# A macaron layer on one core: row statistics, one residual and three small steps take other places at the stages' changes

## The chip, the cores and the metric

The kernel runs on one core of one Trainium2 chip. Its time is the device time of one execution in microseconds (us). Five engines work side by side, each with a queue of its own that is served in order: TensorE (PE, matrix multiplies and transposes), VectorE (DVE), ScalarE (ACT), GpSimd (POOL) and SyncE (SP, which here only issues DMAs). They wait for one another by semaphores, and the program writes every wait by hand. The matrix products are float32 products made of three products of a high and a low half each.

## The reference

Input x has 8 batches of 1024 rows of 128 features (8192 rows).

```python
x = x + 0.5 * ffn(layernorm(x), ...)      # mixture of 16 experts, the best 4 by row, and a shared one
x = x + attn(layernorm(x), w_q, w_k, w_v) # rotary, causal, 1 head of 128, per batch of 1024 rows
x = x + 0.5 * ffn(layernorm(x), ...)      # the same weights again

# ffn: scores = sigmoid(x @ gate_w.T); the top 4 of scores + gate_b; their scores normed, times 2.5
#      y = sum over e of c_e * ((silu(x @ w1_e.T) * (x @ w3_e.T)) @ w2_e.T), plus the shared expert
# layernorm: (x - mean) / sqrt(var + 1e-5), over the 128 features
```

## The kernel before

The layer runs as three stages on the whole core: the first ffn over 16 tiles of 512 rows (T = 0 to 15), attention over 8 batches of 8 query blocks of 128 rows, the second ffn over 16 tiles (T = 16 to 31 in the semaphores' counts). Features lie on the partitions in the ffns, rows in attention.

A tile of an ffn is nine steps j: eight pairs of experts and the shared expert. In step j TensorE makes the gate product and the up product of pair j (`ffn_up`, three 512-column matmuls each) and, three steps behind, the down product of pair j-3 (`ffn_down`). ScalarE takes silu of the gate, VectorE multiplies it by the row weights (`ffn_weighted`, L1316) and by the up product (`ffn_h`, L1326), ScalarE rounds that to the high half (`ffn_h_hi`, L857) and GpSimd subtracts it for the low half (`low_half`, L633). A gate product waits until `ffn_weighted` of two steps earlier has left its PSUM bank, an up product until `ffn_h` has left its own.

Beside that each tile prepares the next ones. The sums of a tile's rows and of their squares (mean and variance) come three or four tiles ahead, from VectorE (`ffn_stats`, `ffn_mv`) or, for most tiles, from ScalarE (`ffn_means`, `ffn_vars`, L885 and L894). GpSimd makes the root (`ffn_rows`) and takes the mean off (`ffn_center`), VectorE scales (`ffn_scale`, L1203), ScalarE and VectorE split it (`ffn_xh`, `ffn_xl`, L1196), and TensorE makes the router's logits of the next tile (`ffn_logitsT`). ScalarE copies them out (`ffn_logitsT` of its own), VectorE chooses the experts and transposes the weights (`ffn_combT`, L1305), and SP writes these to DRAM and loads them back, spread over all partitions, by ten DMAs per tile in five groups (`comb_rows`, L462 and L473). `ffn_weighted` waits for the group that holds its pair.

The opening (tile 0) is written out by hand in `ffn_start` of each engine and the `start` branches of `ffn_tile`: weights are still split, row weights of the first four pairs go by `comb_spread` over TensorE, and TensorE fills waits with multiplies of zeros (`warm`). TensorE runs gates 0 to 5, then the logits of tile 1. VectorE makes the statistics of tiles 0 to 3, that of tile 3 between `ffn_xl` of tile 1 and `ffn_weighted` 2.

In tile 14 the first batch of attention is prepared: GpSimd makes root and shift (`attn_shift`, four operations) behind the low half of step 2, ScalarE applies them to eight blocks (`attn_xn`, L955), two blocks a step in steps 4 to 7, and TensorE transposes the first four (L2075) in step 6.

In attention, query block i of a batch goes through scores, `attn_max` (L1668, VectorE), `attn_exp` (ScalarE), `attn_probT` (TensorE transposes, ScalarE copies), `attn_pv` (TensorE) and `attn_residual` (L1679, VectorE). `attn_pv` of block i waits for `attn_residual` of block i-1. In the last batch the routing of the second ffn's first tile (T = 16) runs between these steps on VectorE (`ffn_prep`), and `ffn_combT` of that tile ends it.

## Time and profile before

| | us |
|---|---|
| median of three runs | 816.37 |
| lowest, highest | 814.94, 819.16 |
| the profiled execution's own time | 816.33 |
| its span (first to last instruction) | 814.5 |
| TensorE busy | 802.5 (99%) |
| VectorE busy | 722.9 (89%) |
| GpSimd busy | 615.2 (76%) |
| ScalarE busy | 600.1 (74%) |

The span divides into the first ffn (to about 312 us), attention (to about 510 us) and the second ffn. A matmul of 512 columns is drawn with a length of 0.39 us while the next one starts 0.23 us behind it, so "busy" is close to full even where a short wait stands between two of them; the timeline's bracket gives only the part of a wait that lies beyond the drawn end.

### The profile page before, as it was taken

The page shows a single profiled execution, that of the slowest core. Times are in us where ns is not written, and L with a number is a line of the kernel's source. Part 1 is how long each engine was busy: PE and PEld are TensorE (multiplying, and loading weights), DVE is VectorE, ACT ScalarE, POOL GpSimd, SP SyncE. Part 2 cuts the span into 40 slices and gives each one's busy share as a digit, 9 for nine tenths or more (in the row PEclk, how much of TensorE's full clock was granted, in tenths as well). Part 3 has the DMA queues.
Part 4 walks back from the last instruction along what each step waited for, and adds up shares of the span by engine and source line. Part 5 has one row for each costly group of instructions (what it writes and reads, how often), then busy time and mean ns, then how long its engine had stood idle before and what let it go on. Part 6 is the DMA issues. An engine that isn't in the chain of part 4 may idle for free. (4 is left out here: it accounts for less than half of the span.)

```text
span 814.5 us, 15848 instructions
## 1 busy us (share of the span) xinstructions
PE 802.5 (99%) x4066; PEld 657.1 (81%) x4066; DVE 722.9 (89%) x2027; ACT 600.1 (74%) x1495; POOL 615.2 (76%) x560
## 2 busy tenths in 40 slices
PE   8999999999999999999999999999999999999998
PEld 7677777777778767899999998777777777777887
DVE  6899999999999988788888888789999999999986
ACT  5777788888786677776676766778788778886664
POOL 6777777777777679888888884477777777777764
PEclk9999999999999999999999999999999999999999
DMA  7567788878877746643333450556676776666653
GB/s 231 137 175 210 211 246 237 243 233 243 219 207 209 206 123 163 159 140 83 100 96 112 145 150 20 159 148 188 183 201 194 195 202 197 179 177 173 184 143 94
DMA packets 93480, 140.83 MB, mean 173 GB/s; under 512 B 10352, under 2 KB 39648, under 8 KB 93408
## 3 DMA queue, kind: packets, MB, share of 16 engines
q1 hardware_dynamic: 93408, 140.03, 61.6%
q8 instruction: 25, 0.41, 0.2%
q14 instruction: 47, 0.39, 0.1%
HBM read 112.67 MB, written 18.93 MB: 162 GB/s over the span
## 5 line engine op out<-in xcount | busy, mean ns | idle before, releaser
L633 POOL TENSOR_TENSOR h_l<-probT,h_h 128x512 fp32r<-128x512 f32 x254 | 330.0, 1302 | 137.4 <-ACT h_h L857 135.1
L857 ACT ACTIVATE h_h<-probT 128x512 fp32r<-128x512 f32 (+1 forms) x285 | 179.4, 629 | 58.2 <-DVE probT L1326 28.6
L1798 PE MATMUL bank<-xh,w_h 128*128 128x512 f32 x545 | 218.7, 401 | 2.4 <-DVE prob L1316 1.4
L1798 PE MATMUL bank<-xh,w_l 128*128 128x512 f32 x545 | 214.2, 393 | 0.0
L1798 PE MATMUL bank<-xl,w_h 128*128 128x512 f32 x545 | 213.8, 392 | 0.0
L920 ACT ACTIVATE bank<-bank 128x512 f32<-128x512 f32 x252 | 146.2, 580 | 68.5 <-PE bank L1798 65.9
L1326 DVE TENSOR_TENSOR probT<-prob,bank 128x512 f32<-128x512 f32 x255 | 172.6, 677 | 15.3 <-POOL h_l L633 3.6
L1316 DVE TENSOR_TENSOR prob<-bank,qkT 128x512 f32<-128x512 f32 x252 | 171.3, 680 | 15.6 <-ACT bank L920 11.2
L1798 PEld LDWEIGHTS bank<-xh,w_h 128*128 128x128 f32 x545 | 102.3, 188 | 40.5 <-DVE probT L1329 7.2
L1798 PEld LDWEIGHTS bank<-xh,w_l 128*128 128x128 f32 x545 | 102.3, 188 | 23.3
L1798 PEld LDWEIGHTS bank<-xl,w_h 128*128 128x128 f32 x545 | 102.3, 188 | 21.2
L1798 PE MATMUL bank<-h_h,w_h 128*128 128x512 f32 (+1 forms) x297 | 113.7, 388 | 0.2 <-POOL h_l L633 0.2
L1798 PE MATMUL bank<-h_h,w_l 128*128 128x512 f32 (+2 forms) x297 | 113.8, 388 | 0.0
L1798 PE MATMUL bank<-h_l,w_h 128*128 128x512 f32 (+1 forms) x264 | 101.0, 387 | 0.0
L857 ACT ACTIVATE probT<-bank 128x512 f32<-128x512 f32 (+2 forms) x96 | 44.4, 489 | 49.2 <-PE bank L2124 49.2
L1798 PE MATMUL bank<-stage,probT 128*128 128x128 f32 x576 | 76.4, 278 | 0.8 <-DVE X L1679 0.5
L1798 PEld LDWEIGHTS bank<-stage,probT 128*128 128x128 f32 x576 | 70.8, 191 | 5.8 <-DVE X L1679 1.8
L1798 PEld LDWEIGHTS bank<-h_h,w_h 128*128 128x128 f32 x297 | 55.5, 188 | 16.8 <-POOL h_l L633 1.5
L1798 PE MATMUL bank<-qkT 128*128 128x512 f32 (+4 forms) x288 | 65.3, 353 | 0.5 <-issue 0.5
L1798 PEld LDWEIGHTS bank<-h_h,w_l 128*128 128x128 f32 (+1 forms) x297 | 55.2, 188 | 11.0
L1798 PEld LDWEIGHTS bank<-h_l,w_h 128*128 128x128 f32 x264 | 49.2, 188 | 10.6
L633 POOL TENSOR_TENSOR qkT<-rot,qkT 128x512 fp32r<-128x512 f32 x32 | 43.5, 1371 | 11.5 <-ACT qkT L857 11.5
(143 smaller groups left out, 1340.5 us busy)
## 6 DMA issues: line engine op xcount, KB each, us to landing
qkT<-comb_rows SPq DMA_DIRECT2D x190, 256.0 KB, 5.2
qkT<-comb_rows SPq DMA_DIRECT2D x124, 128.0 KB, 3.0
rows<-comb_rows SPq DMA_DIRECT2D x28, 512.0 KB, 7.1
stage<-stage SPq DMA_DIRECT2D x64, 128.0 KB, 3.0
X<-in_x SPq DMA_DIRECT2D x16, 256.0 KB, 3.1
stage<-in_x_t SPq DMA_DIRECT2D x16, 256.0 KB, 6.7
x_t<-stage SPq DMA_DIRECT2D x16, 256.0 KB, 4.5
X<-x_rows SPq DMA_DIRECT2D x64, 64.0 KB, 5.8
```

The costliest lines, as they stand in the source:

```text
L633: nc.gpsimd.tensor_tensor(lo, f, hi.bitcast(F32), ALU.subtract).then_inc(done, 1)
L857: return nc.scalar.activation(dst, src, ACT.Copy)
L920: nc.scalar.activation(bank[:, G_BANK[g], :], bank[:, G_BANK[g], :], ACT.Silu).then_inc(silu_done, 1)
L1316: nc.vector.tensor_tensor(weighted[j % 2], bank[:, G_BANK[(q + j) % 2], :], comb_b[q][:, j, :], ALU.mult).then_inc(weighted_done, 1)
L1326: nc.vector.tensor_tensor(h_place(T, q, j), weighted[j % 2], bank[:, u, :], ALU.mult).then_inc(h_done, 1)
L1798: return nc.tensor.matmul(dst, lhsT, rhs, start=start, stop=stop)
```

## The change

- Opening: the statistics of tile 3 leave VectorE. ScalarE makes its means between the copy of the down weights and `comb_spread(2)`, and its variances in two halves around the copy of tile 1's logits. They go to a small tile of their own, `mv_3`. TensorE takes tile 1's logits ahead of gate 5 instead of behind it.
- End of tile 0: VectorE makes `ffn_xl` of tile 2 ahead of its product of step 8, not behind it.
- Tile 14: `attn_shift` stands behind the low half of step 1, not 2, and `attn_xn` runs in steps 3 to 6, not 4 to 7.
- Last batch of attention, i = 6: `attn_residual` of block 5 stands ahead of `attn_max` of block 7.
- Second ffn's first tile: the statistics of tile 3 of that ffn (T = 19) are made before the tile, between `attn_scale` and `attn_residual`, not in it.

```diff
--- before.py
+++ after.py
@@ -135,6 +135,7 @@
 
         stats = sb("stats", [P, QB, 6])
         mv = sb("mv", [P, QB, 2])
+        mv_3 = sb("mv_3", [P, NB, 2])
         var_eps = sb("var_eps", [P, QB])
         rstd = sb("rstd", [P, QB])
         neg_one = sb("neg_one", [P, QB])
@@ -407,11 +408,17 @@
 
         def stats_count(T, base):
 
-            return T - (13 if base else -1)
+            return T - (14 if base else -1)
 
         def means_count(T, base):
 
-            return T - (7 if base else 3)
+            return T - (6 if base else 2)
+
+        def tile_mv(T, base):
+
+            if isinstance(T, int) and T == 3 and not base:
+                return mv_3[:]
+            return mv[:, NB * (T % 2):NB * (T % 2 + 1)]
 
         block = ctx.enter_context(nc.Block())
 
@@ -632,14 +639,14 @@
             def low_half(lo, f, hi, done):
                 nc.gpsimd.tensor_tensor(lo, f, hi.bitcast(F32), ALU.subtract).then_inc(done, 1)
 
-            def ffn_var(T, at, base):
+            def ffn_var(T, at, base, src):
 
                 pool.wait_ge(mv_done, ln_count(T, base))
-                nc.gpsimd.tensor_tensor(var_eps[:, at], mv[:, at, 1], eps[:, at], ALU.add).then_inc(var_done, 1)
+                nc.gpsimd.tensor_tensor(var_eps[:, at], src[:, :, 1], eps[:, at], ALU.add).then_inc(var_done, 1)
 
             def ffn_rstd(T, base=0):
                 at = slice(NB * (T % 2), NB * (T % 2 + 1))
-                ffn_var(T, at, base)
+                ffn_var(T, at, base, mv[:, at])
                 nc.gpsimd.tensor_tensor(neg_mean[:, at], mv[:, at, 0], neg_one[:, at], ALU.mult).then_inc(neg_mean_done, 1)
                 pool.wait_ge(var_done, pool_count(T, base))
                 nc.gpsimd.tensor_tensor(rstd[:, at], var_eps[:, at], neg_half[:, at], ALU.pow).then_inc(rstd_done, 1)
@@ -659,10 +666,11 @@
             def ffn_rows(T, q, base):
 
                 at = slice(NB * q, NB * (q + 1))
-                ffn_var(T, at, base)
+                src = mv_3[:] if isinstance(T, int) and T == 3 else mv[:, at]
+                ffn_var(T, at, base, src)
                 wait(pool, combT_done, T - 2)
-                scale = root_d[:] if not isinstance(T, int) or T - base >= TURN_AHEAD else neg_one[:, at]
-                nc.gpsimd.tensor_tensor(comb[:, :, NEXP], mv[:, at, 0], scale, ALU.mult).then_inc(neg_mean_done, 1)
+                scale = root_d[:] if not isinstance(T, int) or T == 3 or T - base >= TURN_AHEAD else neg_one[:, at]
+                nc.gpsimd.tensor_tensor(comb[:, :, NEXP], src[:, :, 0], scale, ALU.mult).then_inc(neg_mean_done, 1)
                 pool.wait_ge(var_done, pool_count(T, base))
                 nc.gpsimd.tensor_tensor(comb[:, :, NEXP + 1], var_eps[:, at], neg_half[:, at], ALU.pow).then_inc(rstd_done, 1)
 
@@ -706,7 +714,7 @@
                         low_half(h_l[k][:], h[g], h_h[k][:], h_lo_done)
                     else:
                         low_half(h_h[k][INTER:P, :], h[g][0:INTER, :], h_h[k][0:INTER, :], h_lo_done)
-                    if j == 2 and first_batch == 0:
+                    if j == 1 and first_batch == 0:
                         attn_shift(0, rstd, neg_shift)
                     elif j == PAIRS - 2 and first_batch == 0:
                         attn_shift(1, rstd_1, neg_shift_1)
@@ -882,7 +890,7 @@
                 act.wait_ge(mv_done, ln_count(T - 1, base))
                 for n in (2 * part, 2 * part + 1):
                     x = row_block(Tx, n) if base else raw_block(Tx, n)
-                    ins = nc.scalar.activation(unused[:, n, :, :], x, ACT.Identity, scale=MEAN_SCALE, accum_out=mv[:, NB * q + n, 0:1])
+                    ins = nc.scalar.activation(unused[:, n, :, :], x, ACT.Identity, scale=MEAN_SCALE, accum_out=tile_mv(T, base)[:, n, 0:1])
                 if part:
                     ins.then_inc(means_done, 1)
 
@@ -891,8 +899,8 @@
                 act.wait_ge(means_done, means_count(T, base))
                 for n in (2 * part, 2 * part + 1):
                     x = row_block(Tx, n) if base else raw_block(Tx, n)
-                    ins = nc.scalar.activation(unused[:, n, :, :], x, ACT.Square, bias=mv[:, NB * q + n, 0:1], scale=DEV_SCALE,
-                                               accum_out=mv[:, NB * q + n, 1:2])
+                    ins = nc.scalar.activation(unused[:, n, :, :], x, ACT.Square, bias=tile_mv(T, base)[:, n, 0:1], scale=DEV_SCALE,
+                                               accum_out=tile_mv(T, base)[:, n, 1:2])
                 if part:
                     ins.then_inc(mv_done, 1)
 
@@ -983,7 +991,9 @@
                     elif not start or j >= SPREAD:
                         ffn_silu(T, q, j)
                     if start and j == 3:
+                        ffn_vars(3, 3, 1, 0, base)
                         ffn_logitsT(T + 1, base)
+                        ffn_vars(3, 3, 1, 1, base)
                     if j >= NB and j < PAIRS and (t is None or t + TURN_AHEAD < TILES):
                         if j == NB and not base:
                             act.wait_ge(x_next[q], 16 * (2 * turn + c // 2 + 1))
@@ -1000,7 +1010,7 @@
                         ffn_logitsT(T + 1, base)
                     if j == (3 if first else 2) and not last:
                         ffn_gsilu(T + 1)
-                    at = j - (UNITS - 1 - NB)
+                    at = j - (UNITS - 2 - NB)
                     if 0 <= at < NB and first_batch == 0:
                         attn_xn(0, 2 * at)
                         attn_xn(0, 2 * at + 1)
@@ -1033,6 +1043,9 @@
                         ffn_xn(base + 1, 1, n)
                     act.wait_ge(w2_loaded, 16)
                     copy(w2_h[:], w2_f).then_inc(w2_hi, 1)
+                    act.wait_ge(x_loaded[3], 16)
+                    ffn_means(3, 3, 1, 0, base)
+                    ffn_means(3, 3, 1, 1, base)
                     comb_spread(2)
                     opening_xh(1, 1)
                     ffn_silu(base, 0, 3)
@@ -1418,13 +1431,7 @@
                         ffn_weighted(T, q, j)
                         ffn_h(T, q, j)
                     ffn_xl(N, 1 - q)
-                    dve.wait_ge(x_loaded[3], 16)
-                    ffn_stats(L, Lx, 1 - q)
                     ffn_weighted(T, q, 2)
-                    ffn_stats_wait(L)
-                    dve.wait_ge(var_done, 1)
-                    dve.wait_ge(neg_mean_done, 1)
-                    ffn_mv(L, 1 - q)
                     ffn_h(T, q, 2)
                     ffn_logits_turn(N, base)
                     ffn_logit0(N)
@@ -1449,8 +1456,8 @@
                             ffn_combT(N, 1 - q, True, base)
                         ffn_h(T, q, j)
                     ffn_scale(T + 2, base)
+                    ffn_xl(T + 2, q)
                     ffn_h(T, q, PAIRS)
-                    ffn_xl(T + 2, q)
                     return
                 if last:
                     for j in range(PAIRS):
@@ -1472,16 +1479,11 @@
                     ffn_h_lo(T, q, PAIRS, h_lo_done)
                     return
                 late = 1 if first else 0
-                if first:
-                    ffn_stats(L, Lx, 1 - q)
-                    ffn_stats_wait(L, base)
                 for j in range(PAIRS):
                     step = j - late
                     ffn_weighted(T, q, j)
                     if j == 0 and first_batch == 0:
                         attn_ln(0, 2)
-                    elif j == 0 and first:
-                        ffn_mv(L, 1 - q)
                     if step == 1:
                         ffn_logit0(N)
                     elif step == 2:
@@ -1737,6 +1739,8 @@
                         attn_rrow(b, p, i - 1)
                     elif not first:
                         attn_rrow(b - 1, 1 - p, QB - 1)
+                    if last and i == QB - 2:
+                        attn_residual(b, p, i - 1)
                     if i + 1 < QB:
                         attn_max(b, i + 1)
                     elif not last:
@@ -1751,7 +1755,8 @@
                     elif not last and i == 0:
                         attn_scale(b + 1, 0)
                     if i >= 1:
-                        attn_residual(b, p, i - 1)
+                        if not last or i != QB - 2:
+                            attn_residual(b, p, i - 1)
                     elif not first:
                         attn_residual(b - 1, 1 - p, QB - 1)
                     if last and i >= 1:
@@ -1787,7 +1792,10 @@
             attn_rrow(B - 1, 1, QB - 1)
             dve.wait_ge(combT_done, TILES + 1)
             attn_scale(B, 1)
+            ffn_stats(TILES + 3, 3, 1)
             ffn_xl(TILES + 1, 1)
+            ffn_stats_wait(TILES + 3, TILES)
+            ffn_mv(TILES + 3, 1)
             attn_residual(B - 1, 1, QB - 1)
             ffn(TILES)
 
@@ -1863,8 +1871,8 @@
                 pe.wait_ge(w13_split[2], 1)
                 start_gate(4)
                 start_u(4)
+                ffn_logitsT(1, 1)
                 start_gate(5)
-                ffn_logitsT(1, 1)
                 comb_spread(3)
                 pe.wait_ge(w2_split, 1)
                 pe.wait_ge(weighted_done, 2)
```

## Rows read from the trace of the kernel before

**Rows 1.** Busy time by stretch, the body of the first ffn: bounds; length, each engine, clock.

```profile
80.00:300.00 220.00, 218.97 (x939) 172.08 (x938) 207.31 (x576) 168.91 (x433) 166.91 (x155) 1.00 0.77 219
```

**Rows 2.** Timeline, opening, TensorE: start, length, what, idle before and releaser.

```profile
26.02 2.50 PE L1798 MATMUL bank<-X 128*128 128x128 f32 x20 [0.39 <-DVE prob L1311]
...
31.46 0.50 PE L1798 MATMUL bank<-xh,w_h 128*128 128x512 f32 x1 [0.30 <-DVE prob L1316]
...
36.87 0.40 PE L1798 MATMUL bank<-xh,w_l 128*128 128x512 f32 x1
...
38.21 0.42 PE L1798 MATMUL bank<-xh,gw_hl 128*32 128x512 f32 x1 [0.94 <-DVE xl L1196]
```

**Rows 3.** Timeline, opening, ScalarE.

```profile
17.59 0.63 ACT L857 ACTIVATE cos<-comb 128x512 f32<-128x512 f32 x1 [0.76 <-DVE comb L1294]
...
23.07 1.10 ACT L857 ACTIVATE logitsT<-bank 32x128 f32<-32x128 f32 x4 [1.57 <-PE bank L1798]
...
26.04 0.30 ACT L885 ACTIVATE prob<-X 128x128 f32<-128x128 f32 x1
...
31.02 0.38 ACT L894 ACTIVATE prob<-X,mv 128x128 f32<-128x128 f32 x1
...
35.66 0.60 ACT L857 ACTIVATE xh<-bank 128x512 fp32r<-128x512 f32 x1 [0.34 <-DVE bank L1203]
```

**Rows 4.** Timeline, opening, VectorE.

```profile
21.31 0.86 DVE L1366 BATCH_NORM_STATS2 stats<-X 128x6 f32<-128x128 f32 x4
...
24.21 0.31 DVE L1214 STREAM_TRANSPOSE logits<-logitsT 128x128 f32<-128x128 f32 x1 [0.58 <-ACT logitsT L857]
...
37.46 0.69 DVE L1196 TENSOR_TENSOR xl<-bank,xh 128x512 fp32r<-128x512 f32 x1
```

**Rows 5.** Line 1203 (the scaling), whole span: shortest, median, longest in ns, starts.

```profile
L1203 DVE TENSOR_TENSOR bank<-xn,rows x28: 694/1164/1184, 34.9 to 770.7; 128x512 f32<-128x512 f32 x28
```

**Rows 6.** Timeline, tile 14 and the start of tile 15, four engines.

```profile
285.85 1.30 POOL L633 TENSOR_TENSOR h_l<-probT,h_h 128x512 fp32r<-128x512 f32 x1 [0.69 <-ACT h_h L857]
...
285.95 0.58 ACT L920 ACTIVATE bank<-bank 128x512 f32<-128x512 f32 x1 [0.18 <-PE bank L1798]
...
288.25 0.68 DVE L1316 TENSOR_TENSOR prob<-bank,qkT 128x512 f32<-128x512 f32 x1
...
289.47 0.88 ACT L955 ACTIVATE xn<-X,neg_shift,rstd 128x128 f32<-128x128 f32 x2 [0.87 <-POOL neg_shift L763]
...
290.87 0.69 DVE L1316 TENSOR_TENSOR prob<-bank,qkT 128x512 f32<-128x512 f32 x1 [0.77 <-ACT bank L920]
...
292.30 0.63 PE L2075 MATMUL bank<-ident,xn 128*128 128x128 f32 x4 [0.55 <-ACT xn L955]
...
299.11 0.47 PE L1798 MATMUL bank<-xh,wqkv 128*128 128x512 f32 x1 [0.25 <-DVE xl L1628]
```

**Rows 7.** Timeline, last query blocks and the second ffn's first tile.

```profile
505.69 1.50 PE L1798 MATMUL bank<-stage,probT 128*128 128x128 f32 x12
...
506.86 1.22 DVE L1668 CUSTOM_DVE_ANT_0 bank<-bank,mask 128x1024 f32<-128x1024 f32 x1
...
508.41 1.81 PE L1798 MATMUL bank<-stage,probT 128*128 128x128 f32 x14 [0.45 <-DVE X L1679]
...
508.53 1.12 ACT L1102 ACTIVATE prob<-bank,negmax 128x1024 f32<-128x1024 f32 x1
...
509.24 0.31 DVE L1305 STREAM_TRANSPOSE combT<-comb 128x128 f32<-128x128 f32 x1
...
512.31 0.69 DVE L1196 TENSOR_TENSOR xl<-bank,xh 128x512 fp32r<-128x512 f32 x1 [0.94 <-ACT xh L857]
...
515.92 0.69 DVE L1316 TENSOR_TENSOR prob<-bank,qkT 128x512 f32<-128x512 f32 x1 [0.41 <-DMA qkT<-comb_rows]
...
516.67 0.50 PE L1798 MATMUL bank<-xh,w_h 128*128 128x512 f32 x1 [0.54 <-DVE prob L1316]
...
520.13 0.69 DVE L1316 TENSOR_TENSOR prob<-bank,qkT 128x512 f32<-128x512 f32 x1 [0.66 <-DMA qkT<-comb_rows]
```

## The prediction

> **What bounds the kernel.** I read the busy time by stretch first: through the body of the first ffn TensorE is busy for 218.97 of 220 us at a granted clock of 1.00 (2.4 GHz), a matmul each 220/939 = 0.234 us, with VectorE at 207.31 [rows 1]. So TensorE sets the time, and an edit is worth what it takes out of TensorE's few waits, or puts in. Next comes TensorE's timeline: the reader is to see that its waits stand almost only in the opening [rows 2], at the end of the first ffn [rows 6] and between the last query blocks and the next ffn's start [rows 7]. Last come the timelines of the engines that end those waits. A bracket there is short by the drawn tail: the logits at 38.21 follow a matmul at 36.87, so the true loss is 38.21 - 36.87 - 0.23 = 1.11, not 0.94 [rows 2].
>
> Durations are those of the profiled execution: 816.33 us, of which 814.5 are span and 1.8 lie around it. The median of the runs is 816.37, so what is subtracted from one holds for the other.
>
> **Opening, statistics and logits.** VectorE loses four statistics of 0.86 us together [rows 4] and four aggregates, which are shorter. That alone brings nothing: the next thing on VectorE is the router's transpose at 24.21, which waits for ScalarE's copies, begun at 23.07 and 1.10 long, and ScalarE idled 1.57 us for TensorE's logits before them [rows 3, 4]. The logits move ahead of gate 5, so three matmuls of 0.23 = 0.69 earlier, and the copies start at 22.38. For that `ffn_xl` of tile 1 must be ready: it ends at 21.31 plus a small overlap, about 21.4, and TensorE comes to the logits at about 21.7. The waits do not change in kind.
>
> ScalarE's new work is 4 means and 4 variances. The first two variances (two starts 0.39 apart and a read of the accumulator, about 0.87) [rows 3] begin where the engine fell idle, 23.07 - 1.57 = 21.50, and end at 22.4: hidden. The other two end at 23.4 + 0.8 = 24.2, where the high half of step 2 began before anyhow, since it stood behind the copies that are now earlier. The four means begin 0.76 before 17.59, at 16.83, and need 4 x 0.29 + 0.1 = 1.3 us, so `comb_spread(2)` starts about 0.5 late and ends at 18.7; TensorE takes it up at 18.9, after its transposes. Hidden by 0.1 to 0.2; without that cover it costs up to 0.5. GpSimd needs the sums at 26.1 and has them at 24.2.
>
> So VectorE runs 0.69 earlier from the transpose on. TensorE's waits at 26.02 and 31.46 end with VectorE's multiplies by the weights; the zeros begin at most 0.39 + 0.16 = 0.55 earlier (TensorE has nothing left to wait for), and the gates at 28.8 and 31.46 follow VectorE by 0.69. TensorE is 0.69 early at the end of the opening, at 36.87 - 0.69 + 0.23 = 36.41.
>
> **Tile 0, `ffn_xl` before the product of step 8.** The split of tile 2 now follows ScalarE's high half at once. That one ended at 35.66 + 0.60 = 36.26, now 35.57; the split takes 0.69 and ends at 36.30 instead of 38.15 [rows 3, 4]. TensorE's logits start when it is there itself, at 36.41: 38.21 - 36.41 = 1.80 us gained by these two parts together, my value. The product of step 8 ends near 37.0 and is wanted by gate 1 at 37.6; cover 0.6. Bounds: if `comb_spread(2)` loses its cover, 1.3; if the split comes late by 0.5 as well, 0.9; above, all four true waits of the opening (0.55, about 0.45, 0.46, 1.11) gone, 2.6. The body of the ffn has TensorE busy throughout, and VectorE has 12.7 us of 220 free to follow [rows 1], so I keep the 1.80 to the end.
>
> The scaling that feeds this split took 0.694 us here, the shortest of 28, whose median is 1.164 [rows 5]. It began 0.04 us ahead of a GpSimd low half. If the two start in the other order it costs 0.47, the split ends at 36.78 and the gain is 1.38. The Trainium skill, "SBUF — State Buffer", section "SBUF: two separate sides", says that VectorE with two SBUF inputs and a GpSimd operation that reads SBUF share a port pair under an exclusive lock, and whichever starts first holds it for its whole instruction. By that rule the split's time hangs on which of the two comes first by hundredths; the spread of rows 5 agrees, and all of it is inside my bounds.
>
> **Tile 14, shift and normalised blocks one step earlier.** TensorE's transpose at 292.30 waited for `attn_xn`, a true loss of 0.72. `attn_xn` waited for GpSimd's shift, which stood behind a low half of 1.30 us that itself began after 0.69 idle. Moved ahead of it, the shift is ready 1.99 us earlier, and `attn_xn` can start at 287.48 instead of 289.47 [rows 6]. But it now stands in step 3, ahead of silu 4 on ScalarE, which ran at 285.95. ScalarE waits from 285.8 to 287.5, then two blocks (0.79), and silu 4 ends at 288.27 + 0.57 = 288.84. VectorE's multiply 4 goes from 288.25 to 288.88, 0.63 late, and fills the 0.77 that VectorE idled before multiply 5. On ScalarE follow the high half of step 3 and two more blocks, and silu 5 starts at 290.1 instead of 290.26: multiply 5 at 290.72 instead of 290.87. TensorE's gate 6 and up 6 lose about 0.35 to the late multiply and product 4, its transpose comes at 292.06. From multiply 5 on it is VectorE that runs without a gap and releases TensorE's later waits, that at 299.11 for one. So the 0.72 taken away is late again there, and the stage gains only VectorE's 0.15. Bounds: gain 0.72 (all kept), loss 0.3 (up 6 late and nothing returned). The delayed low half of step 2 ends at 288.71, wanted at 288.79: 0.08 of cover, 0.1 lost if it is gone.
>
> **Last batch, residual ahead of the maximum.** The wait removed is that before 508.41: the PV product of block 6 could have started at 507.72, 0.69 earlier. The residual of block 5 needs the PV product of block 5, which ends at 505.69 + 1.50 = 507.19, and starts 0.12 behind it, at 507.30; VectorE, free at 506.86, stands until then. The maximum slips by 507.30 + 0.27 - 506.86 = 0.71, and what is queued behind both by 0.71 less the 0.27 that the residual no longer takes there: 0.44. The maximum ends at 508.84, so the exponential begins at 508.88, not 508.53, and the transposes of block 7, which began at 510.06 behind the PV product, now wait for it until about 510.1. The 0.69 is gone two instructions later. And `ffn_combT` of T = 16, at 509.24, slips to 509.68. Its DMAs are the chain that the next ffn's opening hangs on: multiply 0 at 515.92 and multiply 2 at 520.13 both waited for them, and TensorE at 516.67 waited for multiply 0 [rows 7]. VectorE runs without a gap from multiply 2 to the next tile's weights, whose DMAs again hold two multiplies, so the shift goes through: a loss of 0.44. Bounds: gain 0.69 if the DMAs' landing does not follow their issue; loss 0.7 if they fall badly.
>
> **Statistics of T = 19.** 0.86 us in the 0.94 that VectorE idled before the split at 512.31, the aggregates in the next idle stretch before the residual [rows 7]. Taken out of the tile, they free VectorE in front of the DMA wait at 515.92, where it idled 0.41 already, and once between multiply and product 0, where nothing waits long. Worth 0; bounds 0.3 either way.
>
> **Sum.** -1.80 - 0.15 + 0.44 + 0 = -1.51, so 816.33 - 1.51 = 814.8.
>
> **Rivals.**
> All removed waits stay removed: -1.80 - 0.72 - 0.69 = -3.21, 813.1. For it: each has a bracket in TensorE's row. Against: rows 6 and 7 show the next release on VectorE or a DMA, close behind.
> The opening gives less: the scaling meets the low half, or the means push `comb_spread(2)`; gains of 1.38 to 0.9, mean 1.1: 815.5. For it: 0.04 us of order, 0.1 of cover. Against: both chains shift alike.
> Slower: the lead of 1.80 is given back in the first ffn, because VectorE, 94% busy there (207.31 of 220), releases TensorE at tile 14's end whatever TensorE's lead; its place is the run of VectorE from multiply 5 in tile 14, its price the whole 1.80. Then -0.15 + 0.44 is left: 816.6. It decides once VectorE's own shift there is under 0.3. Against: VectorE lost over 1 us of work in the opening and its multiplies wait for TensorE's gates, so it comes earlier too.
>
> **Chances and range.** Forecast 0.50, rival one 0.15, two 0.19, three 0.12, something else 0.04. The terms' bounds give 816.33 - 2.6 - 0.72 - 0.69 - 0.3 = 812.0 and 816.33 - 0.9 + 0.3 + 0.7 + 0.3 = 816.7; three runs of one kernel lay between 814.94 and 819.16. The range is 813.0 to 817.0. A measurement tells about 0.5% from no change, 4.1 us; no sum of bounds goes beyond that by more than 0.3, so faster 0.04, same 0.93, slower 0.03.
>
> **What would show it.** Logits of tile 2 at 36.4 with no bracket, TensorE's waits near 25.5 gone; silu 4 of tile 14 some 2.3 late against its gate, transposes without a wait, the wait before the first query product still there; the transposes of block 7 waiting for ScalarE; and combT to multiply 0 as long as before (6.68), with TensorE's wait of about 0.7 to 1.1 grown. Wrong if the first ffn's end has not moved by 1.5 or more, if the weights' DMAs do not follow combT, or if a new wait of over 0.5 stands in the body of an ffn.

## The result

| | before | after |
|---|---|---|
| median of 15 runs each, us | 816.61 | 818.10 |
| lowest, highest | 812.97, 819.16 | 816.73, 819.10 |
| the profiled execution's own time | 816.33 | 817.25 |
| its span | 814.5 | 815.5 |

The ratio is 1.0023, 95% interval [1.0014, 1.0033]: the kernel became 0.2% slower, within the 0.5% that the prediction called no change, but beyond its range and on the other side of its forecast of 814.8.

### The profile page after: what moved, and what is told of

It is laid out like the page before. It is cut to its first block, busy times and chain, and to the rows that moved or that the text cites. A ratio compares the mean times of both kernels' runs of the same rounds, so it can differ in the third digit from the quotient of the medians.

```text
span 815.5 us, 15856 instructions
## 1 busy us (share of the span) xinstructions
PE 804.9 (99%) x4066; PEld 659.2 (81%) x4066; DVE 726.4 (89%) x2019; ACT 600.0 (74%) x1511; POOL 613.9 (75%) x560
## 4 chain that ended last, share of the span: by engine, by line
PE 59%; DVE 2%; DMA 1%; POOL 1%; issue 0%; SPq 0%; ACT 0%; DVEq 0%; ACTq 0%; POOLq 0%
PE bank L1806 55%; PE bank L2132 4%; DMA qkT<-comb_rows 0%; DMA comb_rows<-combT 0%; DMA stage<-stage 0%; DVE bank L1670 0%; DVE prob L1329 0%; SPq L480 0%; POOL rstd L768 0%; DVE probT L1339 0%; DVE bank L1655 0%; POOL h_h L640 0%; POOL h_l L640 0%; DVE rope_c L1636 0%; PE bank L2156 0%
## 5 line engine op out<-in xcount | busy, mean ns | idle before, releaser
L1806 PE MATMUL bank<-xh,w_l 128*128 128x512 f32 x545 | 216.6, 397 | 0.0
```

What stands on the lines that cost most here:

```text
L1806: return nc.tensor.matmul(dst, lhsT, rhs, start=start, stop=stop)
```

## The profile after

The body of the first ffn looks the same as before by stretch (length; each engine's busy us and instructions; clock), and is the counterpart of [rows 1]. TensorE's busy time even rose by 0.4 us.

```profile
80.00:300.00 220.00, 219.40 (x940) 172.65 (x939) 208.35 (x575) 167.75 (x432) 166.59 (x155) 1.00 0.76 218
```

The difference shows only from start to start. Each of the next two fences has the first and the last of 35 matmuls of 512 columns that follow one another without a wait, within one tile (timeline, TensorE: start, length, what). The kernel before:

```profile
150.05 0.39 PE L1798 MATMUL bank<-xl,w_h 128*128 128x512 f32 x1
...
157.88 0.39 PE L1798 MATMUL bank<-xh,w_h 128*128 128x512 f32 x1
```

The kernel after:

```profile
150.00 0.39 PE L1806 MATMUL bank<-xh,w_h 128*128 128x512 f32 x1
...
157.95 0.40 PE L1806 MATMUL bank<-xh,w_l 128*128 128x512 f32 x1
```

34 steps take 7.83 us before and 7.95 after: 230.3 and 233.8 ns each. Over all starts from 60 to 270 us that are less than 260 ns apart (some 890 of each trace) the mean is 230.97 before and 233.71 after, at a granted clock of 1.00 in both. The drawn lengths, 0.39 and 0.40, hide it.

By tile, from the logits of tile 8 to those of tile 11, before and then after:

```profile
148.50 0.39 PE L1798 MATMUL bank<-xh,gw_hl 128*32 128x512 f32 x1
...
203.57 0.40 PE L1798 MATMUL bank<-xh,gw_hl 128*32 128x512 f32 x1
```

```profile
148.13 0.39 PE L1806 MATMUL bank<-xh,gw_hl 128*32 128x512 f32 x1
...
203.53 0.39 PE L1806 MATMUL bank<-xh,gw_hl 128*32 128x512 f32 x1
```

Three tiles take 55.07 us before and 55.40 after: 18.36 and 18.47 each. Each tile has 79 matmuls in both traces. 79 of 233.7 ns are 18.46 us, so after the change TensorE never waits in these tiles. 79 of 231.0 are 18.25; before, a tile held about 0.11 us of short waits, which absorbed part of the difference. An undisturbed tile thus takes 0.11 us more, in the second ffn by somewhat less (mostly 18.47, not 18.33 to 18.42); an estimate for some 30 tiles is 3.3 us. The lead of the opening is eaten by that: TensorE was 0.87 us ahead at the logits of tile 2 and 0.36 at those of tile 15 (277.73 before, 277.37 after), 0.18 behind at those of T = 16 and 1.0 at the end. These two traces show less than 3.3 us because the profiled execution of before had four longer waits, of 0.29, 0.63, 0.70 and 0.43 us, in the ffns' bodies, 2.05 in all, that after has not: from the logits of T = 17 to those of T = 31 it took 258.73 us before and 258.79 after.

Those four waits are DMAs that landed late, not part of the change. GpSimd waited for the transposed rows in `stage` ahead of three of them, VectorE 0.57 us for row weights ahead of the fourth. GpSimd's timeline, the kernel before:

```profile
141.96 1.31 POOL L680 TENSOR_TENSOR xn<-stage,rows 128x512 f32<-128x512 f32 x1 [0.48 <-DMA stage<-in_x_t]
...
216.06 1.31 POOL L680 TENSOR_TENSOR xn<-stage,rows 128x512 f32<-128x512 f32 x1 [0.89 <-DMA stage<-in_x_t]
...
731.09 1.31 POOL L680 TENSOR_TENSOR xn<-stage,rows 128x512 f32<-128x512 f32 x1 [0.60 <-DMA stage<-x_t]
```

The opening, timeline of the kernel after. TensorE, beside [rows 2]:

```profile
25.39 2.40 PE L1806 MATMUL bank<-X 128*128 128x128 f32 x20
...
28.07 0.50 PE L1806 MATMUL bank<-xh,w_h 128*128 128x512 f32 x1 [0.28 <-DVE prob L1329]
...
30.73 0.50 PE L1806 MATMUL bank<-xh,w_h 128*128 128x512 f32 x1 [0.29 <-DVE prob L1329]
...
36.23 0.40 PE L1806 MATMUL bank<-xh,w_l 128*128 128x512 f32 x1
...
37.34 0.42 PE L1806 MATMUL bank<-xh,gw_hl 128*32 128x512 f32 x1 [0.71 <-DVE xl L1209]
```

ScalarE, beside [rows 3]:

```profile
17.68 0.62 ACT L865 ACTIVATE cos<-comb 128x512 f32<-128x512 f32 x1
...
22.35 1.10 ACT L865 ACTIVATE logitsT<-bank 32x128 f32<-32x128 f32 x4
...
35.96 0.60 ACT L865 ACTIVATE xh<-bank 128x512 fp32r<-128x512 f32 x1 [1.53 <-PE bank L1806]
```

VectorE and GpSimd, beside [rows 4, 5]:

```profile
23.48 0.31 DVE L1227 STREAM_TRANSPOSE logits<-logitsT 128x128 f32<-128x128 f32 x1 [0.75 <-ACT logitsT L865]
...
34.14 1.72 DVE L1216 TENSOR_TENSOR bank<-xn,rows 128x512 f32<-128x512 f32 x1
...
36.59 0.69 DVE L1209 TENSOR_TENSOR xl<-bank,xh 128x512 fp32r<-128x512 f32 x1 [0.72 <-ACT xh L865]
```

```profile
34.01 1.30 POOL L640 TENSOR_TENSOR h_l<-probT,h_h 128x512 fp32r<-128x512 f32 x1 [0.51 <-ACT h_h L865]
```

Up to 34 us it went as worked out: logits copied out at 22.35 (22.38 forecast), the transpose 0.73 earlier, the zeros without a wait; TensorE is done with the opening's products at 36.23 + 0.23 = 36.46. Then the scaling took 1.72 us. A GpSimd low half had started 0.13 us before it and ended at 35.31; 0.55 us later the scaling was done. In the kernel before the order was the other one, the scaling from 34.87 to 35.56 and the low half 0.04 us behind it, and there it was the low half that took long, 1.80 us instead of 1.30:

```profile
34.91 1.80 POOL L633 TENSOR_TENSOR h_l<-probT,h_h 128x512 fp32r<-128x512 f32 x1 [0.68 <-ACT h_h L857]
```

So after the change the split ended late and the logits came at 37.34 with 0.88 us truly lost.

Tile 14, after, beside [rows 6], ScalarE, VectorE and TensorE in turn:

```profile
286.99 0.88 ACT L963 ACTIVATE xn<-X,neg_shift,rstd 128x128 f32<-128x128 f32 x2 [1.70 <-POOL neg_shift L771]
287.78 0.58 ACT L928 ACTIVATE bank<-bank 128x512 f32<-128x512 f32 x1
```

```profile
288.39 0.69 DVE L1329 TENSOR_TENSOR prob<-bank,qkT 128x512 f32<-128x512 f32 x1 [0.54 <-ACT bank L928]
```

```profile
290.40 0.50 PE L1806 MATMUL bank<-xh,w_h 128*128 128x512 f32 x1 [0.30 <-DVE probT L1339]
...
291.90 0.60 PE L2083 MATMUL bank<-ident,xn 128*128 128x128 f32 x4
...
298.69 0.47 PE L1806 MATMUL bank<-xh,wqkv 128*128 128x512 f32 x1 [0.23 <-DVE xl L1630]
```

ScalarE waits 1.70 us for the shift with silu 4 behind it, up 6 waits 0.30, the transposes wait for nothing, and the wait before the first query product is still there: as forecast.

The last batch and the second ffn's first tile, after, beside [rows 7], TensorE, ScalarE and VectorE:

```profile
505.88 1.50 PE L1806 MATMUL bank<-stage,probT 128*128 128x128 f32 x12
...
508.59 1.80 PE L1806 MATMUL bank<-stage,probT 128*128 128x128 f32 x14 [0.45 <-ACT probT L865]
...
517.20 0.50 PE L1806 MATMUL bank<-xh,w_h 128*128 128x512 f32 x1 [0.56 <-DVE prob L1329]
```

```profile
507.85 0.98 ACT L865 ACTIVATE probT<-bank 128x512 f32<-128x512 f32 x2 [1.52 <-PE bank L2132]
...
509.24 1.11 ACT L1115 ACTIVATE prob<-bank,negmax 128x1024 f32<-128x1024 f32 x1 [0.41 <-DVE negmax L1670]
```

```profile
507.48 0.35 DVE L1681 SCALAR_TENSOR_TENSOR X<-bank,rrow,X 128x128 f32<-128x128 f32 x1 [0.38 <-PE bank L1806]
...
507.92 1.23 DVE L1670 CUSTOM_DVE_ANT_0 bank<-bank,mask 128x1024 f32<-128x1024 f32 x1
...
510.09 0.31 DVE L1318 STREAM_TRANSPOSE combT<-comb 128x128 f32<-128x128 f32 x1
...
516.45 0.69 DVE L1329 TENSOR_TENSOR prob<-bank,qkT 128x512 f32<-128x512 f32 x1 [1.21 <-DMA qkT<-comb_rows]
```

The PV product of block 6 starts 2.71 us behind that of block 5, as before (2.72), but the releaser named has changed: it is now the first of ScalarE's two copies of the transposes of block 6, drawn from 507.85 to 508.45. Before, the same copies began as late against the PV product of block 5 (1.98 us behind it, now 1.97):

```profile
507.67 0.98 ACT L857 ACTIVATE probT<-bank 128x512 f32<-128x512 f32 x2 [1.52 <-PE bank L2124]
```

The first of them ended at 508.26 and the residual at 508.34, so either would have held the product, which starts 0.14 to 0.15 us behind that copy's end in both traces. `combT` starts 4.21 us behind the PV product of block 5, before 3.55. Multiply 0 follows `combT` by 6.36 us, before by 6.68. The statistics of T = 19 stand at 511.43 in the gap ahead of the split of 512.80.

## The experiments

The first theory was that `mv_3`, 32 bytes per partition allocated behind `mv`, moves every tensor behind it, TensorE's operands among them, and that this sets the spacing. The rival was that the new order of the work does. Ratios are against the kernel before on the same chip; where no ratio stands there was one execution, whose time alone says little (the kernel before itself lay between 812.97 and 819.16 us) and whose trace is what counts. "Spacing" is the mean worked out as above. It repeats well: the eight traces in which no tensor was moved have 230.91 to 230.99 ns, on at least three chips.

**The kernel before plus 32 unused bytes.**

```diff
         mv = sb("mv", [P, QB, 2])
+        spare = sb("spare", [P, NB, 2])
```

> The kernel before, with one unused tile of 32 bytes per partition allocated behind mv, where the change put mv_3; no instruction differs, but every tensor allocated later, the matmuls' moving operands among them, lies 32 bytes further on. Theory A (placement: the 32 bytes slow the matmuls): in the body of the first ffn the starts of 512-column matmuls lie 233 to 234 ns apart as in the changed kernel, not 231 as before, the short waits of the kernel before are gone from the body, a tile takes 18.47 us instead of 18.36, and the time is 1 to 3.5 us over the kernel before. Theory B (order of work: the spacing comes from the moved statistics, logits and splits): spacing 231 ns and the time of the kernel before, within 0.7 us. Theory C (chance of one execution or chip): spacing unrelated to the kernel.

Ratio 1.0043 [1.0028, 1.0059], 818.56 us; spacing 233.71 ns. The same two logits as above, TensorE's timeline:

```profile
149.23 0.39 PE L1799 MATMUL bank<-xh,gw_hl 128*32 128x512 f32 x1
...
204.63 0.39 PE L1799 MATMUL bank<-xh,gw_hl 128*32 128x512 f32 x1
```

Again 55.40 us for three tiles, without any of the moves. Unused bytes alone cost at least about as much as the whole change did (the two intervals overlap).

**All of the change, mv_3 allocated last.**

> The changed kernel whole, but mv_3 is the last tensor allocated, so all others lie where the kernel before has them. Theory A (placement): spacing 231 ns in the body as before, and what the moves themselves bring is left: with the opening's measured 0.87 us of lead and some loss at the last query blocks, 1.5 us under to 0.5 us over the kernel before, in any case 1.5 to 4 us under the changed kernel. Theory B (order of work): spacing 233 to 234 ns and the time of the changed kernel, 1.3 to 2.0 us over the kernel before.

Ratio 1.0002 [0.9989, 1.0014]; spacing 230.99, logits of tile 2 at 37.45. The placement is shown from both sides, and it also shows that the moves together were worth nothing that this measurement tells.

**All of the change, 64 bytes on instead of 32** (a second tile of 32 bytes beside `mv_3`).

> The changed kernel with a second unused tile of 32 bytes beside mv_3, so that all later tensors move by 64 bytes against the kernel before. If what counts is where in a 64-byte line an operand begins, it is as the run with mv_3 last: spacing 231 ns, a time 1.5 to 4 us under the changed kernel. If any move of the operands costs, or the order of work does, spacing 233 to 234 ns and 1.3 to 2.0 us over the kernel before.

Ratio 1.0010 [0.9997, 1.0023]; spacing 232.40, tile 18.41 us. Neither back to 231 nor left at 233.7, as neither theory had it: a return after 64 bytes is refuted by the spacing. The time, not told from that of the kernel before, does not say it.

**The kernel before, once more.**

> The kernel before once more, for a second profile of it. Theories A and B: spacing 231 ns in the body again, tiles of 18.36 us, and some tiles of 18.6 to 19.1 us again. Theory C (chance): another spacing, 233 to 234 ns as likely as not.

813.99 us, span 812.2, spacing 230.93, tiles 18.36. The waits of the opening and of the last batch stand where they stood; single waits of 0.3 to 0.7 us in the ffns' bodies (the profiled run of before had them between the logits of tiles 7 and 8, 11 and 12, 24 and 25, 28 and 29) stand in other tiles. They make up the 2.3 us between the spans of these two executions of one kernel: 0.42 in tiles 3 to 15, 1.92 from T = 17 to T = 31. In all 20 traces of this case together 16 tiles between the logits of tiles 3 and 15 took over 18.6 us; in 14 of them GpSimd waited 0.23 to 1.58 us for a DMA of transposed rows, in one VectorE waited 0.86 for row weights, and one stays open. With 32 bytes more behind `mv` there was none in the first ffn's body.

**The residual's move alone**, on the kernel before.

```diff
+                    if last and i == QB - 2:
+                        attn_residual(b, p, i - 1)
                     if i + 1 < QB:
                         attn_max(b, i + 1)
```

> The kernel before with one move of the change: in the last batch of attention the residual of block 5 ahead of the maximum of block 7. Theory R (the waits there are given by other engines): TensorE's wait before the PV product of block 6 stays at 0.69 us, because ScalarE's copy of the transposes ends just as late; the maximum slips 0.9 to 1.1 us, the transposes of block 7 wait for the exponential, the transpose of the routing weights of tile 16 slips by 0.5 to 0.7 us, and the multiply that waits for its DMAs and TensorE's gate behind it slip by as much; time 0.3 to 0.8 us over the kernel before, hardly to be told from none by the runs. Rival (the change's own aim): the 0.69 goes, combT slips at most 0.44, time equal or up to 0.7 us less.

Ratio 1.0000 [0.9985, 1.0016]. TensorE's and VectorE's timelines:

```profile
507.89 1.80 PE L1801 MATMUL bank<-stage,probT 128*128 128x128 f32 x14 [0.45 <-ACT probT L857]
```

```profile
506.78 0.35 DVE L1679 SCALAR_TENSOR_TENSOR X<-bank,rrow,X 128x128 f32<-128x128 f32 x1 [0.35 <-PE bank L1801]
...
509.21 0.31 DVE L1305 STREAM_TRANSPOSE combT<-comb 128x128 f32<-128x128 f32 x1
```

The wait before the PV product of block 6 stays at its old length under a new releaser, and `combT` slips by 0.49 us (4.04 behind the product of block 5, at 505.17, not 3.55). The prediction had the slip at 0.44 and this run's expectation at 0.5 to 0.7; the gain of 0.69 two instructions earlier never came about. The maximum slipped by 0.71 (1.88 behind the product of block 5, not 1.17), as the prediction had it and less than the 0.9 to 1.1 expected here, and the loss of 0.3 to 0.8 us expected on the whole kernel is not told from none.

**The opening's moves alone**, `mv_3` last.

> The kernel before with the opening's moves alone (statistics of tile 3 on ScalarE, logits of tile 1 ahead of gate 5, the split of tile 2 ahead of product 8), mv_3 allocated last. Theory P (the scaling meets GpSimd's low half): the scaling at 34.1 us takes about 1.7 us, TensorE still waits 0.9 us (true loss) for the split and the logits of tile 2 start at 37.3 to 37.5 instead of 38.2, a lead of 0.75 to 0.9 us that lasts to the end: time 0.7 to 0.9 us under the kernel before. My forecast before the result: 36.4, a lead of 1.8. Rival: the lead is given back in the first ffn, time equal to before.

Ratio 0.9982 [0.9968, 0.9996]; logits of tile 2 at 37.38 after the scaling of 1.72 us. The four traces with this opening have them at 37.33 to 37.45, ten of the old opening at 38.02 to 38.40. Four more of the old opening have them at 38.63 to 39.36: there ScalarE waited 1.8 to 2.5 us, not the 1.34 of before, for the DMA of weights `stage<-in_w13T`. So one trace of the opening can be 1.2 us late by a DMA alone, and it is the repetition that shows the lead.

**The change without the residual's move, the scaling of tile 2 a step earlier**, `mv_3` last.

```diff
+                        if j == PAIRS - 1:
+                            ffn_scale(T + 2, base)
                         ffn_h(T, q, j)
-                    ffn_scale(T + 2, base)
                     ffn_xl(T + 2, q)
```

> The changed kernel with mv_3 allocated last, the residual of block 5 back in its old place, and in tile 0 the scaling of tile 2 put ahead of product 7, so that it runs before GpSimd begins its low half. Theory P: the scaling takes 0.7 us, ScalarE's high half of the split is set by its own queue, the logits of tile 2 start at 36.4 to 36.7 with at most 0.2 us of wait, a lead of 1.5 to 1.8 us over the kernel before; time 1.2 to 2.0 us under the kernel before and under every version so far. Rival: the scaling's length does not hang on what GpSimd does beside it, it takes 1.2 us or more again and the logits start at 37 or later.

Ratio 0.9971 [0.9956, 0.9987], 814.66 us: faster than both kernels. VectorE, GpSimd and TensorE:

```profile
33.45 0.70 DVE L1216 TENSOR_TENSOR bank<-xn,rows 128x512 f32<-128x512 f32 x1
...
35.02 0.69 DVE L1209 TENSOR_TENSOR xl<-bank,xh 128x512 fp32r<-128x512 f32 x1 [0.28 <-ACT xh L865]
```

```profile
34.10 1.30 POOL L640 TENSOR_TENSOR h_l<-probT,h_h 128x512 fp32r<-128x512 f32 x1 [0.51 <-ACT h_h L865]
```

```profile
36.48 0.40 PE L1804 MATMUL bank<-xh,gw_hl 128*32 128x512 f32 x1
```

Ahead of the low half the same instruction takes 0.70 us, and the logits of tile 2 start without a wait, 1.73 us earlier than before: nearly the 1.80 that the prediction gave the opening.

**128 and 192 unused bytes behind `mv`; 32 bytes behind `xl`; the tile-14 move alone; the opening with the early scaling and nothing else.** The first three are the kernel before with a larger `spare` at its place, or with `spare` ahead of `away0`. The fourth is:

```diff
-                    if j == 2 and first_batch == 0:
+                    if j == 1 and first_batch == 0:
                         attn_shift(0, rstd, neg_shift)
...
-                    at = j - (UNITS - 1 - NB)
+                    at = j - (UNITS - 2 - NB)
```

> The kernel before with an unused tile of 128 bytes behind mv. So far, with mean spacing of 512-column matmuls in the body of the first ffn: shift 0: 230.95 ns; 32 bytes: 233.71; 64 bytes: 232.40. If the spacing repeats with the position in a 128-byte line, 231.0; if any shift from the old place costs, 232 to 234.

> The kernel before with an unused tile of 192 bytes per partition behind mv. With 0, 32, 64 and 128 bytes the mean spacing of 512-column matmuls in the first ffn was 230.95, 233.71, 232.40 and 232.76 ns. If the place counts modulo 64 bytes: 230.95 (already unlikely by 64 and 128); modulo 128: as 64, 232.4; without such a period: anything from 231 to 234, span 812 to 818.

> The kernel before with an unused tile of 32 bytes per partition between xl and the router's tiles, so that xh, xl and xn stay where they were and h_h, h_l, stage and qkT lie 32 bytes further on. By the theory that it is the place of the operand which a matmul reads that sets its spacing: products of xh and xl as before (229.5 to 231.4 ns), those of h_h and h_l as in the changed kernel (233.5, 230.3, 231.9 against 230.2, 232.6, 232.9 before), which is nothing on the mean: 231 ns, span 812 to 815. By the rival that it is the number of bytes allocated ahead of the last tensors, or the place of what the other engines read: 233.7 ns, span about 817.

> The kernel before with the tile-14 move alone (attn_shift behind the low half of step 1, attn_xn in steps 3 to 6), no tile moved. By the prediction's step it is worth 0.15 us, by its upper bound 0.72, by its lower -0.3: ratio 1.000 within 0.0015, and the transposes of step 6 of tile 14 without a wait while a later wait grows. The rival that the whole wait removed is kept gives 0.9991.

> The changed kernel without the tile-14 move, the residual's move and the statistics of T = 19, mv_3 allocated last, and the scaling of tile 2 in tile 0 ahead of the product of step 7. If only the opening's moves and the early scaling bring something, this is as fast as the run with all moves but the residual (ratio 0.9971): 0.996 to 0.998, span about 812.5. If the tile-14 move or the statistics brought part of that, it is 0.1% slower.

128 bytes: 819.12 us, spacing 232.76. 192 bytes: 815.22, spacing 231.65. Behind `xl`: 821.04, spacing 232.76, with products of `xh` and `w_h`, neither of which had moved, at 232.0 ns, not 229.5. It had 25 starts more than 260 ns apart; the longest of them, and with them its long time in the first ffn, come from four late loads of transposed rows, 3.85 us of GpSimd's waiting in all. GpSimd's timeline, the longest:

```profile
180.36 1.29 POOL L681 TENSOR_TENSOR xn<-stage,rows 128x512 f32<-128x512 f32 x1 [1.58 <-DMA stage<-in_x_t]
```

Whether the place of the router's small tiles has a part in these one execution cannot say. So the simple form, that each operand's place sets its own product's time, falls. Tile 14 alone: ratio 0.9984 [0.9970, 0.9999]; the transposes without a wait, and 222.31 us from the logits of tile 15 to those of T = 16, against 222.49 and 222.54 in the two runs of the kernel before. That agrees with the prediction's 0.15, but runs that differ from before by unused bytes alone had 222.29 to 223.07 there, so the size is not shown. The opening with the early scaling: 0.9973 [0.9957, 0.9988], the same as with the tile-14 move and the statistics of T = 19 on top.

**Where the shift begins.** What was still open was which tensors' place matters.

> The kernel before with 32 unused bytes ahead of negmax: prob (silu, weighted) and probT (h in float32), which VectorE and ScalarE write and ScalarE and GpSimd read, lie 32 bytes on; nothing that TensorE or a DMA reads in the first ffn moves. If TensorE's spacing depends on the place of its own operands alone: 230.95 ns, span about 813. If it depends on what other engines touch at the same time: above 231.5 ns.

> As the last, and qkT too, which in the ffns holds the row weights that DMAs write and VectorE reads. TensorE's operands stay. Own operands alone: 230.95 ns. If the writes of the DMAs meet TensorE's reads: above 231.5 ns here and not in the run with the shift from prob.

> As the last, and stage, h_h and h_l too; the router's small tiles, comb and combT stay. If h_h and h_l made the slowdown of the run with the shift from behind xl (232.76 ns): again 232.8, with products of h slower by 3 ns. If the router's small tiles did: 230.95 ns.

> The shift from xh on: all of TensorE's moving operands of the ffns 32 bytes on, xn and the tiles ahead of it stay. If xn (GpSimd and VectorE) plays no part: as with the shift from mv on, 233.7 ns, tile period 18.47 us, no waits in the body. If xn does: other than that by over 0.5 ns.

> The kernel before with 32 unused bytes ahead of stage (in the first ffn it holds the transposed rows that DMAs load and GpSimd reads); h_h and h_l stay. If TensorE's own operands make the step of 1.7 ns: 231.0 ns as with the shift from qkT. If stage makes it: 232.7 ns.

> The same ahead of h_l, so that h_h stays and h_l lies 32 bytes further from it. If every moved operand adds its share to its own products: only products of h_l and those next to them change, 231.3 ns on the mean. If it is the distance between operands that follow one another: products of h_h with w_l, whose successor reads h_l, change by over 2 ns.

Each is the kernel before with 32 bytes more, the tensor allocated last first, so each row moves all that the rows above it move. The weights lie ahead of `mv` and move in none. The columns are worked out from the traces (ns, 60 to 270 us): the mean of all, then the mean from the start of a product of the two named to the next start; the last column is the time from the logits of tile 3 to those of tile 15:

| shift from | mean | xh, w_h | h_h, w_l | tiles 3 to 15, us |
|---|---|---|---|---|
| none (before; once more) | 230.97; 230.93 | 229.5 | 232.6; 231.7 | 221.28; 220.86 |
| prob | 230.93 | 229.5 | 232.2 | 220.66 |
| qkT | 231.12 | 230.0 | 232.9 | 221.23 |
| stage | 230.94 | 229.5 | 232.1 | 221.11 |
| h_l | 232.11 | 232.1 | 236.9 | 221.38 |
| h_h | 232.68 | 232.2 | 235.8 | 220.61 |
| behind xl | 232.76 | 232.0 | 235.8 | 224.75 (late loads) |
| xh | 233.76 | 236.1 | 230.2 | 221.61 |
| mv | 233.71 | 235.7 | 230.2 | 221.54 |

The steps lie at TensorE's own moving operands, h_l and h_h for 1.7 ns and xh with xl for 1.1 more, and nowhere else: neither `prob`, `qkT` (row weights, written by DMAs), `stage`, the router's tiles nor `xn` adds more than 0.2 ns. But a product slows whose own operands have not moved. What it follows matters: with the shift from h_l, products of xh and w_h right behind a product of h_l go from 227.7 ns (shift from `stage`) to 233.2, and those behind a product of xh only from 231.0 to 231.5. And h_h with w_l, whose successor reads h_l, goes from 232.1 to 236.9. That a neighbour's operand counts is what the expectation for h_l called the distance between operands; distance alone is not it, since with the shift from h_h both lie as far apart as before and the product still takes 235.8.

TensorE's timeline, the logits of tiles 8 and 10, with the shift from `qkT` and then from `xh`:

```profile
149.03 0.40 PE L1799 MATMUL bank<-xh,gw_hl 128*32 128x512 f32 x1
...
185.75 0.40 PE L1799 MATMUL bank<-xh,gw_hl 128*32 128x512 f32 x1
```

```profile
149.16 0.39 PE L1799 MATMUL bank<-xh,gw_hl 128*32 128x512 f32 x1
...
186.09 0.39 PE L1799 MATMUL bank<-xh,gw_hl 128*32 128x512 f32 x1
```

36.72 and 36.93 us, 18.36 and 18.47 a tile. With the shift from h_h the spacing is 232.68 and the twelve tiles still take 220.61, no more than before: 79 x 232.68 is 18.38, where the tiles of before took 18.36 with their short waits. So the slower matmuls first fill waits that were there anyhow, and at 233.7 ns there are none left to fill. A sharp limit is not shown: at 232.11 and 232.40 ns the tiles took 18.39 and 18.41.

## Why the prediction was wrong, point by point

**What bounds the kernel: right, and read too coarsely.** TensorE sets the time, but the prediction took "a matmul each 220/939 = 0.234 us" from a stretch that holds waits, those of tile 14 among them, and treated it as a constant. From start to start it was 230.97 ns, and not a constant.

**The step that failed is one the prediction does not have.** It priced every instruction that the diff moves and none of its first line, the allocation of `mv_3`. Alone 32 bytes at that place cost ratio 1.0043, about 3.5 us; in the changed kernel, by 1.0023 with the line and 1.0002 without, 1.7. The intervals, 2.3 to 4.8 and (an estimate from the two ratios' own) 0.4 to 3.0 us, overlap. Without it the time would have been that of the kernel before, 816.33 x 1.0002 = 816.5: inside the range, but 1.7 above the forecast. The points below account for 0.6 to 0.8 of that; the rest is within the noise. The prediction's own first sign of being wrong, a first ffn whose end has not moved by 1.5 us, came true: the logits of tile 15 moved by 0.36.

**Opening, statistics and logits (0.69): right.** The copies, the transpose and the zeros moved by 0.7 and ScalarE's new work was hidden; the means pushed `comb_spread(2)` by 0.09 us only, not 0.5, since they began at 16.52, not 16.83, and took 1.16 to its start, not 1.3.

**`ffn_xl` of tile 2 ahead (1.11): mis-sized.** The named danger, the order of scaling and low half, came out the bad way: both chains did not shift alike, VectorE's gained 0.73 us (34.87 to 34.14), GpSimd's 0.90 (34.91 to 34.01). Its price was 1.72 - 0.69 = 1.03 us, not the 0.47 taken from the median of [rows 5]. In the kernel before 26 of the 28 scalings began 0.68 to 0.90 us behind the start of a low half, which had at most 0.62 us left, and ended some 0.55 us behind its end. The rows thus held no case of a low half only just begun. The lead was 0.87 at tile 2. That is near rival two's condition and its lower end of 0.9, not near 1.38. The Trainium skill, "SBUF — State Buffer", section "SBUF: two separate sides", says that the one of the two that starts second is blocked for the other's whole instruction. The traces agree: 0.13 us behind the low half the scaling ended 0.55 us after it, 0.14 us less than its 0.69 alone, and when it started 0.65 us ahead of it, it took 0.70. It holds the other way round too: the low half that began 0.04 us behind the scaling in the kernel before ended 1.15 us behind it, 0.15 less than its own 1.30. Worked out by that rule the bound is the low half's 1.30 less the head start, about 1.2 us (an estimate), and that, a gain of 0.6 and not 0.9, should have been the term's lower end.

**Tile 14 (0.15): right in kind.** The wait before the transposes went and that before the first query product stayed, under the same releaser; the move alone measured 0.9984 [0.9970, 0.9999], which holds 0.15 us and does not tell it from 0.72.

**Residual ahead of the maximum (+0.44): the loss right, the wait wrong.** The prediction took the residual as the only thing that the PV product of block 6 waited for. ScalarE's first copy ends within 0.08 us of it; the wait of 0.45 stayed. `combT` slipped by 0.49 alone and by 0.66 with the rest. Of this 0.13 (alone: 15.41 us from the logits of T = 16 to those of T = 17, not 15.28) to 0.33 (15.61, and 15.59 with `mv_3` last) reached TensorE there; on the whole kernel alone it is not told from nothing. The prediction also had `combT` to multiply 0 as long as before, 6.68; it was 6.36 in the changed kernel, 6.38 with the residual's move alone and 6.31 in the kernel before once more. In that stretch the row weights go out and come back by DMAs, and its length changed between two executions of one kernel (6.68 and 6.31) by nearly as much as the slip.

**Statistics of T = 19 (0): right by itself.** Without the residual's move the same stretch is 15.28, unchanged. With both it is 0.2 longer than with the residual's alone, which the prediction, taking the steps one by one, did not have. The statistics are not its direct cause: the extra 0.17 us of `combT`'s slip are there before they run, since the maximum of block 7 begins 0.44 us behind the start of the residual (507.48 to 507.92) and with the residual's move alone 0.27 (506.78 to 507.05). What holds it stays open.

**Rival three (lead given back in the first ffn, 816.6)** has the outcome nearest to what came, by another mechanism. In the run with the early scaling the lead was 1.73 at tile 2 and the twelve tiles took 220.20 us, the shortest of all, so nothing was given back.

## What to carry to other kernels

A new small tensor is a change to every tensor allocated behind it. Where one engine is 99% busy, price it: allocate it last, or time the old kernel with the unused bytes alone before crediting or blaming the rest. Where a wait is taken away, look for the second releaser that ends just beside the first, as the copy did here (0.08 us). Where two instructions exclude each other, price the bad order at the whole of the other instruction, not at the median of the rows. Last, where a wait of under 2 us appears in one trace, see whether a DMA ended it, and whether a second trace has it at the same place.

## What the runs showed of the hardware

The distance between two matmuls of 512 columns at full clock depended on where their moving operands lie within the partition: 230.95 ns with no shift, 233.71, 232.40, 232.76 and 231.65 with 32, 64, 128 and 192 bytes (the 64 with the change's moves). No repetition after 32, 64 or 128 bytes fits, and products next to the moved ones changed too. The Trainium skill, "SBUF — State Buffer", section "SBUF: two separate sides", says that at these ports TensorE never waits on anyone. No run here shows it waiting for another engine there, but the place of its own operands moved its pace by 1.2%. What in the memory does that stays open: the runs moved tensors in steps of 32 bytes and did not measure a stream of matmuls by itself. A rival is untested, too: ScalarE, VectorE and GpSimd write these same tensors, and where they write moved with them.
